# Sigmoid replaced by a tangent of the sine's table set, and one block of pair sums moved forward, in a recurrent stage of a fused transformer kernel

## The reference

```python
biv = (einsum('btd,od->bto', x, W_biv) + b_biv).reshape(B, T, nb, 3)
decay = sigmoid(einsum('btd,od->bto', x, W_decay) + b_decay)[..., 0]
inj = (einsum('btd,od->bto', x, W_in) + b_in).reshape(B, T, nb, 3)
def step(h, xs):
    b_t, d_t, u_t = xs
    h_new = d_t[:, None, None] * _rodrigues(b_t, h) + u_t   # rotate the 3-vector h about b_t
    return (h_new, h_new)
_, states = scan(step, h0, xs)                              # 192 steps in a row
```

## Time and profile before

| what | us |
|---|---|
| median of 3 runs | 476.28 |
| lowest and highest of them | 473.53, 476.74 |
| the profiled execution | 471.77 |
| its span (first to last instruction) | 469.9 |
| PE busy | 404.4 (86% of the span) |
| DVE, POOL, ACT busy | 296.3, 223.2, 206.2 |

### The profile page before, as it was taken

One profiled execution on the slowest core, in us unless ns is written; L12 is line 12 of the kernel. 1 busy time (PEld: TensorE's weight loads), 2 busy tenths in 40 slices (PEclk: granted clock), 3 DMA queues, 4 the chain that ended last, 5 costly groups with the idle time before them and its releaser, 6 DMA issues.

```text
span 469.9 us, 10064 instructions
## 1 busy us (share of the span) xinstructions
PE 404.4 (86%) x3477; PEld 321.7 (68%) x3477; DVE 296.3 (63%) x1369; ACT 206.2 (44%) x381; POOL 223.2 (48%) x264
## 2 busy tenths in 40 slices
PE   4797758899768988888878988977999999999991
PEld 4652535646435776777755777933999999999991
DVE  2889999899982443443439446886566555665541
ACT  1179976361661111111114501446466656666550
POOL 3300289999026665666330000335456666656532
PEclk9898969999989999999979999997999999999998
DMA  8629000010142222122149997078233333332322
GB/s 244 76 68 260 5 1 1 2 33 2 34 124 59 67 70 68 59 68 67 43 119 269 239 238 171 2 133 137 56 54 62 45 59 61 62 61 43 51 24 27
DMA packets 39075, 38.32 MB, mean 82 GB/s; under 512 B 7546, under 2 KB 36206, under 8 KB 39026
## 3 DMA queue, kind: packets, MB, share of 16 engines
q1 hardware_dynamic: 27510, 22.15, 20.8%
q0 software_dynamic: 9312, 14.03, 15.4%
q10 hardware_dynamic: 2204, 1.49, 1.1%
HBM read 27.29 MB, written 10.37 MB: 80 GB/s over the span
## 4 chain that ended last, share of the span: by engine, by line
PE 30%; DMA 25%; DVE 12%; ACT 12%; issue 9%; another core or an unknown queue 5%; POOL 5%; POOLq 1%; ACTq 0%; DVEq 0%
DMA out<-a,idxs 22%; PE bank L1918 5%; PE bank L1879 3%; POOL reg L665 2%; ACT xn L793 2%; PE bank L1893 2%; ACT reg L825 2%; DMA a<-expert_rows 2%; PE bank L2127 2%; PE bank L1902 2%; POOL reg L675 1%; ACT reg L977 1%; DVE reg L1521 1%; PE bank L1925 1%
## 5 line engine op out<-in xcount | busy, mean ns | idle before, releaser
L1893 PE MATMUL bank<-reg,xT 64*128 64x128 f32 x1116 | 75.2, 275 | 0.7 <-DVE reg L1506 0.6
L696 POOL DMA_INDIRECT reg<-xn_rows,idxs x62 | 60.6, 977 | 30.2 <-issue 17.5
L716 POOL DMA_INDIRECT out<-a,idxs x31 | 50.2, 1619 | 49.4 <-DMA out<-a,idxs 39.3
L1925 PE MATMUL bank<-reg 64*128 64x192 f32 x744 | 71.3, 323 | 1.1 <-DVE a L1533 1.1
L1893 PEld LDWEIGHTS bank<-reg,xT 64*128 64x128 f32 x1116 | 70.8, 188 | 1.2 <-DVE reg L1506 0.7
L1925 PEld LDWEIGHTS bank<-reg 64*128 64x128 f32 x744 | 65.4, 187 | 1.3 <-issue 1.3
L1009 ACT ACTIVATE reg<-reg 128x1152 f32 x31 | 36.1, 1163 | 30.7 <-PE bank L1925 30.7
L988 ACT ACTIVATE reg<-bank 128x288 f32<-128x288 f32 x31 | 12.7, 410 | 83.1 <-PE bank L1879 69.2
L1532 DVE TENSOR_SCALAR a<-bank,gs 128x192 f32<-128x192 f32 x31 | 13.0, 418 | 54.2 <-PE bank L1925 54.2
L1918 PE MATMUL bank<-reg 96*128 x186 | 36.8, 333 | 10.8 <-DVE reg L1521 10.8
L704 POOL DMA_INDIRECT expert_rows<-a,idx x31 | 30.6, 986 | 29.5 <-DVE a L1530 24.6
(11 more groups left out here) (353 smaller groups left out, 815.5 us busy)
## 6 DMA issues: line engine op xcount, KB each, us to landing
reg<-in_w2b SPq DMA_DIRECT2D x8, 576.0 KB, 9.8
reg<-in_w1b SPq DMA_DIRECT2D x8, 288.0 KB, 9.7
reg<-in_w1a SPq DMA_DIRECT2D x8, 216.0 KB
reg<-in_w2a SPq DMA_DIRECT2D x8, 216.0 KB
xn_rows<-xn SPq DMA_DIRECT2D x4, 384.0 KB, 2.7
reg<-in_w1b SPq DMA_DIRECT2D x8, 192.0 KB, 7.2
xn_rows<-xn SPq DMA_DIRECT2D x1, 1152.0 KB, 7.4
out<-h SPq DMA_DIRECT2D x1, 1152.0 KB, 10.1
```

Of the source, the lines that this page charges most:

```text
L696: pool.indirect_dma_start(xs[:, i % RING, 0:(D, D2)[l]], None, xd[l], bass.IndirectOffsetOnAxis(ap=idxs[:, i:i + 1], axis=0)).then_inc(xs_ ...
L716: pool.indirect_dma_start(out, bass.IndirectOffsetOnAxis(ap=idxs[:, i:i + 1], axis=0), ys[:, i % YRING, :], None, compute_op=ALU.add).then ...
L1893: ins = MM(bank[2 + 2 * p + a][:, c * P:(c + 1) * P], w1r[rs, p, col:col + hc], xT64[rs, p, k, :], start=(c == 0 and k == 0), stop=(c == n ...
L1925: ins = MM(bank[6 + a][:, 0:D], hT2[rs, p, c * P:(c + 1) * P], w2r[rs, p, c * D:(c + 1) * D], start=(c == 0), stop=(c == nhc - 1))
```

## The change

- The decay is evaluated as tanh(x/2) in place of sigmoid(x). Since sigmoid(x) = (1 + tanh(x/2))/2, twice the decay is now the stored value plus 1.
- A Silu of one column is put ahead of the first tanh.
- Chunk 0's twice-decay becomes an Identity with a bias of 1 (from a column of constants). For chunks 1 and 2 POOL adds 1 in place to the 512 columns of their decays (and clamps at 0), between `theta2` of chunk 1 and `theta2` of chunk 2, after a wait for `ev_act` 9 (the last tanh); ACT's second root then waits for `twice_ready`. The diagonal's matmuls take a new constant, `halfI` (minus one half on the diagonal), in place of `negI`.
- The sums of pair block 0 go into bank 0 in place of bank 5, and are issued on PE inside `assemble(2)` ahead of group r = 2; ACT copies the block inside `keep_off(2)` ahead of that group's copy. `patches_back` now waits for that copy and stands directly behind the assembly.

```diff
@@ theta_of
             if c:
-                nc.scalar.activation(S.rd[:, 0], chunk(dec, c), ACT.Sqrt, scale=2.0).then_inc(rd_ready, 1)
+                act.wait_ge(twice_ready, 1)
+                nc.scalar.activation(S.rd[:, 0], chunk(dec, c), ACT.Sqrt).then_inc(rd_ready, 1)
@@ POOL
             theta2(G, pool, link, 1)
+            pool.wait_ge(ev_act, 9)
+            late = dec[:, :, NPATCH:T]
+            G.tensor_scalar(late, late, 1.0, 0.0, ALU.add, ALU.max).then_inc(twice_ready, 1)
             theta2(G, pool, link, 2)
@@ proj_evac
-                                ACT.Sigmoid)
+                                ACT.Tanh, scale=0.5)
@@ ACT
-            nc.scalar.activation(negI, ident, ACT.Copy, scale=-1.0).then_inc(neg_ready, 1)
+            nc.scalar.activation(negI, ident, ACT.Copy, scale=-1.0)
+            nc.scalar.activation(halfI, ident, ACT.Copy, scale=-0.5).then_inc(neg_ready, 1)
             theta_of(act, 0)
+            nc.scalar.activation(scr[:, 0:1], con[:, 0:1], ACT.Silu)
             proj_evac(0, [3])
             act.wait_ge(ev_act, 2)
-            nc.scalar.activation(setA.rd[:, 0], chunk(dec, 0), ACT.Copy, scale=2.0).then_inc(rd_ready, 1)
+            nc.scalar.activation(setA.rd[:, 0], chunk(dec, 0), ACT.Identity,
+                                 bias=con[:, C_ONE:C_ONE + 1]).then_inc(rd_ready, 1)
@@ keep_off (ACT)
+                    if (c, r) == (2, 2):
+                        keep_pairs(0)
                     act.wait_ge(asm_mm, 4 * (c - 1) + 2 + r)
@@ assemble (PE)
-                    MM(pair_of(bk, n), negI, dec2(c, n), start=True, stop=False)
+                    MM(pair_of(bk, n), halfI, dec2(c, n), start=True, stop=False)
                     if r == 2:
+                        if c == 2:
+                            pair_sums(0)
                         pe.wait_ge(diag_ev, c)
@@ PE, behind the assemblies
-            for b, n in enumerate(PBLK):
-                if b == 1:
-                    patches_back()
-                if b == 2:
-                    t_pair(2, 0)
-                    t_pair(2, 1)
+            pe.wait_ge(pair_ready, 1)
+            patches_back()
+            pair_sums(1)
+            t_pair(2, 0)
+            t_pair(2, 1)
+            for b in range(2, len(PBLK)):
+                pair_sums(b)
```

More of the change, by code:

```diff
@@ L237, in build @@
         negI = carve(reg1, P)
+        halfI = carve(reg1, P)
         LW = P + 2 * NE
@@ L264, in build @@
         comp += [of_pairs(setA.v.rearrange("p c a t -> p (c a t)"), 0, PBLK[6])]
-        PAIR_BANK = (5, 6, 7, 4, 5, 6, 7)
+        PAIR_BANK = (0, 6, 7, 4, 5, 6, 7)
         dodd = of_pairs(setA.trig.rearrange("p c a t -> p (c a t)"), 0, PAIRS - NODD)
@@ L360, in build @@
         trig_ready = sem("trig_ready"); seg_ev = sem("seg_ev")
-        m_ready = sem("m_ready"); cs_ready = sem("cs_ready"); w2_ready = sem("w2_ready"); rd_ready = sem("rd_ready"); neg_ready = sem("neg_ready")
+        m_ready = sem("m_ready"); cs_ready = sem("cs_ready"); w2_ready = sem("w2_ready"); rd_ready = sem("rd_ready"); neg_ready = sem("neg_ready"); twice_ready = sem("twice_ready")
         q0_ready = sem("q0_ready"); v_ready = sem("v_ready"); vv_ready = sem("vv_ready"); qk_ready = sem("qk_ready")
@@ L908, in keep_diagonal, with keep_pairs @@
                                      ACT.Copy).then_inc(diag_ev, 1)
+            def keep_pairs(b):
+                act.wait_ge(pair_mm, b + 1)
+                nc.scalar.activation(comp[b].rearrange("p i a r c -> p (i a r c)"), bank[PAIR_BANK[b]][:, 0:48 * PBLK[b]],
+                                     ACT.Copy).then_inc(pair_ready, 1)
             def keep_off(c):
                 for r, (bk, sl) in enumerate(((5, slice(1, 5, 3)), (6, slice(6, 10, 3)), (4, slice(2, 9, 6)))):
+                    if (c, r) == (2, 2):
+                        keep_pairs(0)
                     act.wait_ge(asm_mm, 4 * (c - 1) + 2 + r)
@@ L935, in keep_states @@
                                          ring[g % 2][:, 1:SLOTS:2].rearrange(along), ACT.Copy).then_inc(hist_copied, 1)
[L937 to L941, removed]
             squares_q0(1)
@@ L954, in _ @@
             keep_off(2)
-            keep_pairs(0)
             keep_pairs(1)
@@ L1996, in _, with pair_sums @@
             pe.wait_ge(ev_act, 12)
+            def pair_sums(b):
+                n, i0 = PBLK[b], PAIR0 + 2 * sum(PBLK[:b])
+                bk = bank[PAIR_BANK[b]][:, 0:48 * n]
+                if 1 <= b <= 4:
+                    pe.wait_ge(off_ev if b != 2 else diag_ev, (0, 5, 2, 6, 4)[b])
+                elif b > 4:
+                    pe.wait_ge(pair_ready, b - 3)
+                for k in range(3):
+                    pe.wait_ge(term_ready, 3 * b + k + 1)
+                    MM(bk, ident, term[b % 2][k][:, 0:n].rearrange("p i a r c -> p (i a r c)"), start=(k == 0), stop=False)
+                MM(bk.rearrange("p (i a r c) -> p i a r c", a=NCH, r=3, c=4)[:, :, :, :, 3], ident,
+                   Mt[:, i0 + 1:i0 + 2 * n:2, :, :, 3], start=False, stop=True).then_inc(pair_mm, 1)
             def assemble(c):
```

## The result

Over 20 runs each the changed kernel took 473.06 us (470.25 to 478.0), the kernel before 475.15 (472.02 to 478.13): a ratio of 0.9949, 95% interval 0.9929 to 0.9969, or 2.4 us less (1.5 to 3.4); the two medians are 2.1 apart. The ratio leaves out the execution at 478.0, which was a slow one. The forecast was 2.9 less, within 1%. On a second chip, where both kernels were some 15 us quicker, the ratio was 0.9939 (0.9911 to 0.9968).

What follows compares the result with a forecast made beforehand. The prediction took POOL's chain to bound the mixer's end, DVE's scan close behind. ACT's 2.1 plus POOL's closing idle of 1.0, capped at 2.9 by the scan, took the median 476.28 to 473.4 us; range 469.6 to 476.2.

Steps and rivals of the forecast that it cites:

- the scan still idles ahead of block 0: Sign of being wrong: DVE's scan still waiting for the copy of pair block 0, a wait of 2.03 us before.
- The move: Pair block 0 goes ahead of group r = 2 on PE; POOL's 0.96 idle before its last 27 terms closes: 1.0.
- The thin cover (0.2): Block 0's terms from POOL are ready at 83.6, PE's group r = 1 ends at 83.8, so PE doesn't wait: 0.2.
- The tables: ACT's two table loads at 35.42 and 47.13, 1.28 us each, both go: 2.56, or 2.1 after added work.
- POOL's addition: Adding 1 to 512 columns on POOL takes 1.0 us, between 0.51 and 1.27, and costs nothing at 1.0.
- The two clock branches near 40 us: PE's projections: clock stays full, no ACT stall, gain 2.9 (2 to 1); or clock falls, ACT stands 0.9, gain 2.2.
- the 0.9 of the text: ACT's wait for PE's fifth projection unit at the third copy of L835 if the clock falls: 0.9 us.
- g: ACT's gain: 2.56 for two loads, less 0.20 (Silu), 0.10 (Identity) and 0.20 (`halfI`): 2.1 us.
- The rival with this cause: POOL's addition takes 2.5, holds ACT's second root by 1.4 and leaves g = 0.7: gain 1.7, 474.6 us; chance 0.09.
- DVE's idle ahead of block 0: DVE's scan waits 2.03 us for ACT's copy of pair block 0; 1.99 of it was to go.
- the text's own formula: POOL's last 27 term instructions start earlier by g plus 1.0 (its 0.96 idle closing), up to 2.9 us.
- the cap: Limit set by DVE's scan, which comes 0.55 + 0.37 + 1.99 = 2.9 us earlier.

Runs made afterwards that it cites:

- direct_warm: Changed kernel without POOL's addition (biases on ACT instead), with 32 unused PE matmuls: 0.9894 of the kernel before; direct is the same without those matmuls: 0.9933.
- after_again: The changed kernel itself, unaltered, run and profiled a second time on another chip: ratio 0.9939 to the kernel before.
- after_warm: The changed kernel with 32 matmuls of unused results filling PE's wait before assemble(1): ratio 0.9894 to the kernel before.
- add_twice: The changed kernel with POOL's addition made twice, the second adding 0: ratio 0.9998 to the kernel before.

## Why the prediction was right

The time came as forecast, but the prediction named as a sign of being wrong that "the scan still idles ahead of block 0", and it does, by 1.64. So the number is right and the path to it is right in two parts of four.

**The move: right, at its size.** Forecast: POOL's 0.96 idle closes, 1.0 gained. Measured: 42.5 to 41.5 from A2 to E, in every pair of profiles where the scan isn't the bound. The thin cover (0.2) between POOL's terms and group r = 2 held.

**The tables: right.** Both loads went and 1.28 was the price of each. Without POOL's addition and with the clock kept, S to A1 fell by 2.2 (33.4 to 31.2, direct_warm); the forecast was 2.1, and 2.3 on this scale, since the 0.20 for `halfI` lies ahead of S. direct_warm also pays about 0.2 for its two bias columns. No run is without `halfI`: in the second profile of the changed kernel the squares follow it by 0.20, but in the first they stand 0.56 for DVE behind it, so there it cost nothing. The two clock branches near 40 us had the effects drawn, though PE's gap was 1.7 to 2.3 and not 2.4. Of the nine profiles that have the tanh and no load there, six kept the clock, with gaps of 1.66 to 1.86, and three lost it, with 1.91 to 2.27 (after_again, direct, after_warm), which makes no rule, since the gap of 2.51 in the earlier trace rows kept it; in the five with loads there (gaps of 2.8 to 3.2) it always fell. Where it fell, ACT stood for PE ahead of the third copy of the bivectors:

```profile
48.70 0.59 ACT L842 ACTIVATE reg<-bank 64x512 f32<-64x512 f32 x1 [0.86 <-PE bank L1978]
```

That idle of 0.86 in after_again is the 0.9 of the text.

**POOL's addition: a term of the wrong size.** I took 1.0 between 0.51 and 1.27; it was 1.94, above the upper bound. The bound was the two-input instruction of 512 columns, and it is no bound for one input with two operations. At 1.94 it cost ACT 0.75, which took g from 2.1 to 1.3 (in the branch where the clock is kept). The rival with this cause had 2.5 us and a gain of 1.7; the truth lay between it and the forecast.

**DVE's idle ahead of block 0: wrong.** The text let all but 0.04 of the 2.03 go and so made the scan the bound. 1.64 stayed, for two causes: the addition's 0.75, and the clock in assemble(1), which the sum left out altogether. It took every matmul there at the duration of the one profile. The two causes add up: block 0's copy starts 1.6 earlier after S than before, where the forecast is 4.0 on this scale, and the 2.4 that are missing are 0.75 and 1.6. By the table, 3.2 more us at the lower clock are 1.6 of delay, and between two profiles of the same changed kernel (14.05 and 12.96) this alone moves 1.1 us. That is as large as either half of the change.

**The sum.** With g = 1.3 the text's own formula, g + 1.0 below the cap, gives 2.3. Measured were 2.4 and 2.8. The forecast of 2.9 took the cap, and no profile of the changed kernel reached it: the too small addition made it 0.6 too high, inside the interval of the measurement. Nor do the profiles add up to the 2.3: after the clock's 1.6 and 0.5 they show 0.9 and 1.0 from S to E. That the times came so near to the formula, and to the forecast, is in part luck: about 1.5 us of the gain, or more, stand in no piece that was compared. The text also took 4.8 us as the least that a measurement can tell from no change; 20 executions of each kernel told 2.4 from it, to within 1 us.

**What stays open.** Where the rest of the measured gain lies, the 1.5 us and more above. And whether pulling assemble(1) forward gives some of the gain back to the clock on average. In the profiles without the added matmuls it starts between 61.6 and 65.6 and the clock comes back between 66.6 and 69.8, and the low part is 2.9 and 3.8 in the two with sigmoid, 3.6 to 6.1 in the seven with tanh. Nine profiles, with one or two of each kernel, don't settle either. Nor is the move's own time settled, 0.2 us by its ratio, 0.8 with the matmuls added to both sides, and 1.0 by the profiles.

## What to carry over

Cut a varying profile at a few instructions and compare the pieces: here three causes lay in three pieces, while spans and even medians mixed them. Bound the price of an unseen instruction by rows of its own form (inputs and operations), not by one that looks dearer, and put it where nobody waits: here a bias on instructions that run anyway replaced it. And where PE has stood for some us ahead of a critical group, look at the granted clock before counting instructions; filling the gap gave about as much as the change under study, though the mixer's profile shows only a part of it.

## What was not expected of the hardware

On GpSimd an f32 instruction with one input of 512 columns and two operations on constants takes 1.94 us (1.92 again in add_twice) and 1.51 with one operation, more than two inputs with one operation at 1.27, while L749's 192 columns with two operations, on column operands, take 0.51. The granted clock fell in a wait of PE of 2.42 (after_warm) and held through one of 2.43 at the same place (direct_warm). The mean granted clock of whole executions of one and the same kernel lay between 0.933 and 0.951 over the 20 runs of the changed kernel; at 0.933 it took 478.0 us, at 0.948 to 0.951 between 470.25 and 472.31.
